# Order of the softmax work in a two-branch attention kernel: row maxima per bank, local exp split around the block exps, projection split around the first value group

## The reference

```python
q = rmsnorm(apply_partial_rope((h @ Wq_c @ Wq_up), cos, sin), q_norm_w)      # 16 heads
k_sw = rmsnorm(apply_partial_rope(h @ Wk, cos, sin), k_norm_w)               # one key head
v_sw = h @ Wv
ck = rmsnorm(h.reshape(b, nb, M * HID) @ W_comp, k_norm_w)                   # one key per 16 tokens
c_out = attend(q @ ck * scale, valid, sink, ck)                              # block branch
sw_scores = CAP * tanh((q @ k_sw * scale) / CAP)                             # CAP = 50
sw_out = attend(sw_scores, window of 64 tokens, sink, v_sw)                  # local branch
ao = c_out + sw_out
x = layernorm(h + (ao by groups @ Wg) @ Wo)
out = layernorm(x + x @ ternary(weight).T + bias)
```

## Time and profile before

| | us |
|---|---|
| median of 3 runs | 428.15 |
| the runs | 428.15, 428.4, 423.61 |
| the profiled execution, whole | 426.38 |
| its span, first to last instruction | 424.6 |
| busy: TensorE, VectorE, POOL, ScalarE | 367.8, 326.7, 302.3, 287.3 |
| mean granted TensorE clock, share of full speed | 0.965 |

### The profile page before, as it was taken

How to read it: one execution, slowest core, us unless ns; L and a number is a source line. 1 busy time by engine, 2 the same in 40 slices (tenths; PEclk the granted TensorE clock), 3 DMA queues, 4 the chain that set the end, 5 groups by cost and what they waited for, 6 DMA issues and landing times.

```text
span 424.6 us, 8753 instructions
## 1 busy us (share of the span) xinstructions
PE 367.8 (87%) x3109; PEld 297.5 (70%) x3111; DVE 326.7 (77%) x663; ACT 287.3 (68%) x818; POOL 302.3 (71%) x190
## 2 busy tenths in 40 slices
PE   5995798959979998999999999888889999989781
PEld 5993586656757767787878687767676877768660
DVE  2685789677888889897979787989886998963311
ACT  4557775767695969687777767686967695956200
POOL 1834361266796979798989777897979697986805
PEclk9998899978999999999999999999998999999995
DMA  7994004688756676767567676777676676584330
GB/s 248 316 247 112 1 0 67 233 247 124 124 91 123 100 138 95 130 101 121 106 112 103 107 110 108 114 110 139 97 127 100 115 100 125 87 137 76 47 66 25
DMA packets 150284, 50.20 MB, mean 118 GB/s; under 512 B 138593, under 2 KB 148833, under 8 KB 149985
## 3 DMA queue, kind: packets, MB, share of 16 engines
q1 hardware_dynamic: 149424, 49.32, 62.4%
q10 hardware_dynamic: 816, 0.33, 0.3%
HBM read 11.87 MB, written 4.19 MB: 38 GB/s over the span
## 4 chain that ended last, share of the span: by engine, by line
PE 33%; issue 17%; POOL 17%; DVE 11%; ACT 9%; DMA 7%; SPq 6%; POOLq 0%; ACTq 0%; DVEq 0%
PE PS L664 10%; POOL ao L1196 5%; PE PS L615 5%; POOL room_wg L1206 4%; SPq L373 4%; PE PS L641 3%; ACT room_h L822 3%; DMA aoT<-ao 3%; PE PS L471 3%; PE PS L633 3%; ACT ao L704 3%; PE PS L431 2%; PE PS L581 2%; DVE room_K L1112 2%; DMA room_h<-room_K 2%
## 5 line engine op out<-in xcount | busy, mean ns | idle before, releaser
L1196 POOL TENSOR_TENSOR ao<-room_wg,ao 128x1024 f16<-128x1024 f32 x32 | 68.2, 2132 | 28.0 <-ACT ao L704 27.9
L664 PE MATMUL PS<-V,room_wg 128*128 128x129 f32 x512 | 67.0, 285 | 13.7 <-POOL room_wg L1206 10.2
L664 PEld LDWEIGHTS PS<-V,room_wg 128*128 128x128 f32 x512 | 63.3, 197 | 18.8 <-POOL room_wg L1206 13.5
L1206 POOL TENSOR_TENSOR room_wg<-room_comp,keep 128x1024 f32<-128x1024 f32 x32 | 74.7, 2355 | 1.4 <-ACT room_comp L813 1.4
L822 ACT ACTIVATE room_h<-PS,room_K 128x8 f32<-128x8 f32 (+7 forms) x256 | 70.7, 364 | 1.9 <-DVE room_K L1047 1.7
L822 ACT ACTIVATION_READ_ACCUMULATOR room_h<-PS,room_K 128x1 f32 x256 | 62.4, 250 | 0.0
L633 PE MATMUL PS<-Weff,aoT 128*128 128x256 f16 x512 | 58.5, 273 | 3.8 <-DMA aoT<-ao 3.7
L1212 POOL TENSOR_TENSOR ny<-nx,nu 128x16 f32<-128x16 f32 x16 | 46.8, 2924 | 18.3 <-DVE nx L1023 18.3
L633 PEld LDWEIGHTS PS<-Weff,aoT 128*128 128x128 f16 x512 | 49.6, 98 | 10.8 <-issue 4.8
L1021 DVE TENSOR_REDUCE ssq<-room_wg 128x8 f32<-128x1024 f32 x30 | 36.5, 1220 | 21.9 <-ACT room_wg L773 21.5
L581 PE MATMUL PS<-room_h,kT 128*128 128x512 f16 x192 | 47.9, 391 | 4.2 <-ACT room_comp L809 2.4
(11 more groups left out here) (178 smaller groups left out, 734.5 us busy)
## 6 DMA issues: line engine op xcount, KB each, us to landing
H<-in_L_attn_h SPq DMA_DIRECT2D x4, 512.0 KB, 6.3
room_wg<-in_L_attn_Wg SPq DMA_DIRECT2D x1, 2048.0 KB, 14.7
cw_rows<-staged SPq DMA_DIRECT2D x1, 2048.0 KB, 6.4
CW<-cw_rows SPq DMA_DIRECT2D x1, 2048.0 KB, 7.9
aoT<-ao SPq DMA_TRANSPOSE x128, 2.7
out<-room_wo SPq DMA_DIRECT2D x16, 128.0 KB, 2.0
CW<-in_L_attn_Wq_up SPq DMA_DIRECT2D x2, 512.0 KB, 13.5
room_wo<-in_L_attn_Wo SPq DMA_DIRECT2D x1, 1024.0 KB, 15.2
```

The lines of the kernel that those rows point to most:

```text
L664: last = nc.tensor.matmul(pv, Pm[:, c, 2 * pr:2 * pr + 2, :], V[:, 2 * i + c, :], start=True, stop=True)
L1196: G.tensor_tensor(ao16[:, 1, c, :, :], ao[:, c, :, :], ao16[:, 0, c, :, :], ALU.subtract).then_inc(g_al, 1)
L1206: G.tensor_tensor(Pm[:, c, :, :], E[:, c, :, :], keep[:, :, :], ALU.mult).then_inc(g_mask, 1)
```

## The change

- Row maxima: the reduce is cut in two, `row_max(0)` for bank 4 and `row_max(1)` for bank 5. `row_max(0)` stands ahead of `rope_products(0)`, `row_max(1)` where the whole stood. `p_cs` and `d_cmax` count twice a step.
- ScalarE: the first local exp stays, then come the 16 block exps (the second eight wait for the second maxima), then the second local exp.
- x1's transposition goes from before the local scores to behind the second unit of them, where the step has attention; the narrowing of its tile from before the square to behind the first tanh.
- Projection: the blocks come first, then the high part of 16 - 2g heads, `values(0)`, the high part of the other 2g heads, the low part. In steps without attention all 16 heads come at once.

```diff
-                wait(sp, p_cs, t)
+                wait(sp, p_cs, 2 * t)
...
-                if ffn:
+
+                def norm_T():
                     pe.wait_ge(g_x1, i - 1)
...
                 if ffn and not mid:
+                    norm_T()
                     feed_forward()
...
                         last.then_inc(p_sw, 1)
+                        if ffn and u == 1:
+                            norm_T()
...
-                    last.then_inc(p_cs, 1)
+                        last.then_inc(p_cs, 1)
...
+                def project_blocks():
+
+                    pe.wait_ge(a_ct, t + 1)
+                    if t == 0:
+                        pe.wait_ge(s_cwr, 16)
+                    for g in range(groups(t)):
+                        rows = P - HEADS if g == groups(t) - 1 else P
+                        nc.tensor.matmul(o, PcT[0:rows, g, :], CW[0:rows, TPB * (t // TPB) + g, :],
+                                         start=g == 0, stop=False)
+
+                def project_high(heads):
+
+                    for hd in heads:
+                        if hd == 0:
+                            pe.wait_ge(s_ah, 64 * t + 64)
+                        for wp in range(2):
+                            nc.tensor.matmul(o, aoT[:, 0, hd % 2, hd // 2, :], Weff[:, wp, hd, :],
+                                             start=False, stop=False)
...
                 if proj:
 
                     t = i - 1
+                    ahead = HEADS - 2 * groups(t) if mid else HEADS
...
-                    if not mid:
-                        project_blocks(True, range(groups(t)))
-                    pe.wait_ge(s_ah, 64 * t + 64)
...
+                    project_blocks()
+                    project_high(range(ahead))
...
-                if proj and mid:
+                if proj:
+                    project_high(range(ahead, HEADS))
                     project_low()
-                    project_blocks(False, range(groups(t))).then_inc(p_o, 1)
                 if mid:
                     values(1)
...
                 if front and i < 1:
                     square(i + 1, 0)
-                if ffn:
-                    act.wait_ge(p_xt, i - 1)
-                    narrow(x1T[:, 0, :, :], x1_bank(mid).rearrange("p (k n) -> p k n", k=KC), a_xt)
                 if front:
                     square(i + 1, 1)
+                if ffn and not mid:
+                    feed_forward_high()
...
                                              ACT.Tanh, scale=1.0 / CAP).then_inc(a_tanh, 1)
-                    for c in range(2):
+                        if ffn and u == 0:
+                            feed_forward_high()
+
+                    def local_exp(c):
+
                         act.wait_ge(a_tanh, 4 * i + 2 * c + 2)
                         nc.scalar.activation(E[:, c, :, :], E[:, c, :, :], ACT.Exp, scale=CAP).then_inc(a_es, 1)
+
+                    local_exp(0)
...
-                    act.wait_ge(d_cmax, i + 1)
                     wait(act, p_ct, i)
                     n = SUB * groups(i)
                     for hd in range(HEADS):
+                        if hd % 8 == 0:
+                            act.wait_ge(d_cmax, 2 * i + hd // 8 + 1)
...
                             last.then_inc(a_ec, 1)
+                    local_exp(1)
...
+                def row_max(hf):
+
+                    dve.wait_ge(p_cs, 2 * i + hf + 1)
+                    wait(dve, a_ec, 2 * i)
+                    V_.tensor_reduce(mn[:, 8 * hf:8 * hf + 8], scores(i)[:, hf, :, :], AX.X, ALU.max,
+                                     negate=True).then_inc(d_cmax, 1)
+
+                if mid:
+                    row_max(0)
                 if front:
                     rope_products(0)
                 if first:
                     weights_rest(0)
                 if mid:
-
-                    dve.wait_ge(p_cs, i + 1)
-                    wait(dve, a_ec, 2 * i)
-                    V_.tensor_reduce(mn[:, :].rearrange("p (b a) -> p b a", b=2), scores(i), AX.X, ALU.max,
-                                     negate=True).then_inc(d_cmax, 1)
+                    row_max(1)
                 if front:
                     rope_products(1)
```

More of the change, by code:

```diff
@@ L604, in step @@
                 o = bank(7)[:, 0:HID]
[L606 to L624, removed]
-                    if not mid:
-                        project_blocks(True, range(groups(t)))
-                    pe.wait_ge(s_ah, 64 * t + 64)
-                def project_high():
-                    for hd in range(HEADS):
+                def project_blocks():
[10 more added lines that the diff above has]
+                            pe.wait_ge(s_ah, 64 * t + 64)
                         for wp in range(2):
-                            last = nc.tensor.matmul(o, aoT[:, 0, hd % 2, hd // 2, :], Weff[:, wp, hd, :],
-                                                    start=mid and hd == wp == 0, stop=False)
-                    return last
+                            nc.tensor.matmul(o, aoT[:, 0, hd % 2, hd // 2, :], Weff[:, wp, hd, :],
+                                             start=False, stop=False)
                 def project_low():
@@ L641, in project_low @@
                         last = nc.tensor.matmul(o, aoT[:, 1, hd % 2, hd // 2, :], Weff[:, 0, hd, :],
-                                                start=False, stop=not mid and hd == HEADS - 1)
-                    return last
-                if proj and mid:
[L646 to L649, removed]
+                                                start=False, stop=hd == HEADS - 1)
+                    last.then_inc(p_o, 1)
+                if proj:
+                    t = i - 1
+                    ahead = HEADS - 2 * groups(t) if mid else HEADS
+                    if i == 1:
+                        copied(pe, G_FT)
+                    wait(pe, d_y, t)
+                    project_blocks()
+                    project_high(range(ahead))
                 def values(c):
@@ L791, in step, with feed_forward_high @@
             def step(i, front, mid, proj, ffn):
+                def feed_forward_high():
+                    act.wait_ge(p_xt, i - 1)
+                    narrow(x1T[:, 0, :, :], x1_bank(mid).rearrange("p (k n) -> p k n", k=KC), a_xt)
                 if front and i < 1:
                     square(i + 1, 0)
-                if ffn:
-                    act.wait_ge(p_xt, i - 1)
-                    narrow(x1T[:, 0, :, :], x1_bank(mid).rearrange("p (k n) -> p k n", k=KC), a_xt)
                 if front:
                     square(i + 1, 1)
+                if ffn and not mid:
+                    feed_forward_high()
                 if i == -1:
```

## The result

| | before | after |
|---|---|---|
| median, us | 425.78 (22 runs) | 420.31 (22 runs) |
| lowest and highest, us | 421.28 to 432.4 | 417.04 to 427.62 |
| ratio | | 0.9897, 95% interval 0.9869 to 0.9926 |
| profiled execution, whole and span, us | 426.38 and 424.6 | 425.47 and 423.7 |

The account below looks back on a forecast made before the run. The loop was taken as bound by VectorE, then POOL, with TensorE tied in step 7. Terms -0.8 -0.5 -0.3 -0.5 +0.4 +0.6 = -1.1 us took 428.15 to 427.0 us, range 421.5 to 433.

Parts of the forecast that it names:

- one chain from a value group to the next: Step 3: VectorE, then POOL set the 19.1 us loop; no step of it waits for TensorE except the value group.
- Steps 1, 4 and 10, where a DMA came late too, are held by the mask.: Projection split: no gain counted in these steps, although the transposed ao came late there.
- Late ao: Projection split: blocks fill the wait for transposed ao, so value groups start earlier; -0.8 us in step 2, -0.5 in step 11.
- The stall: Value group's wait for block exps goes: -0.3 us in step 7, -0.5 in step 15, each less 0.2 for moved heads.
- Heads behind the group: Projection split: 0.025 us per group moves behind values(0), counting where y waits for the projection, four steps: +0.4 us.
- VectorE's hold: row_max(0) ahead of rope_products(0) holds VectorE for the first bank's scores: +0.6 us over six steps.
- The move of x1: x1's transposition behind the second score group: 0 taken, bounds 0 and -6.8 us.
- The late mask(1): POOL's mask(1) comes 0.4 to 1.3 us after mask(0) is done, waiting for the later exp; covered by other waits.
- TensorE is the bound: Rival: TensorE's waits for x1, exps and late ao all pay, 415.5 us; chance 0.10.
- The slow-clock rival: Late queries and half-clock scores, as in step 12, cost 2.4 us each; four such steps give 436.6 us; chance 0.08.

Follow-up runs that it names:

- the split alone: Kernel before with only the projection split (blocks first, some high heads and the low part behind the first value group): ratio 0.9962, 422.02 us against 424.93.
- The experiment on the low part alone: Kernel before with one swap: behind the first value group the blocks come before the low part; ratio 0.993.
- split and max+exp: Kernel before with the projection split, row maxima per bank and second local exp behind the block exps, without the move of x1: ratio 0.9878.
- both maxima behind: Changed kernel with both row maxima behind the first rope products, so that VectorE isn't held: ratio 0.9895, 420.19 us.
- the experiment on x1: Kernel before with only x1's transposition behind the second score unit and its narrowing behind the first tanh: ratio 1.0039.
- cover without balance: Like the projection split on the kernel before, but all 16 high heads stay ahead of the first value group: ratio 1.0041, 428.9 us.
- four pairs: All eight combinations of the three parts, four with the projection split against four without: mean 0.96% lower with it.
- max+exp: Kernel before with only the row maxima per bank and the second local exp behind the block exps: ratio 1.0034.
- the split with the exp alone: Kernel before with the projection split and second local exp behind the block exps, one reduce for all maxima: ratio 0.9984.

## Why the prediction was wrong

**One route where there are two.** The forecast followed one chain from a value group to the next: divide(0), query_rest, y, x1, POOL's work, mask(0). That is right for the steps from 3 to 4 and from 9 to 10, which stayed at 19.1 us with every part. There is a second from values(0): the low part, the blocks, values(1), the transposition of the block probabilities, its copy and a square on ScalarE, output_high(1), then POOL's output_low(1) and on. The first value group of step 4 starts at 165.70 us before. Behind it come the wait for the low part of ao, the second value group, y, and output_low(1):

```profile
168.08 1.92 PE L641 MATMUL PS<-Weff,aoT 128*128 128x256 f16 x16 [0.33 <-DMA aoT<-ao]
...
171.57 1.95 PE L664 MATMUL PS<-V,room_wg 128*128 128x129 f32 x16
171.89 0.47 DVE L1126 SCALAR_TENSOR_TENSOR room_wo<-PS,o_inv,H 128x256 f32<-128x256 f32 x1
...
177.07 2.13 POOL L1196 TENSOR_TENSOR ao<-room_wg,ao 128x1024 f16<-128x1024 f32 x1 [0.82 <-ACT ao L704]
```

The two value groups with the split alone:

```profile
164.40 2.05 PE L656 MATMUL PS<-V,room_wg 128*128 128x129 f32 x16 [0.76 <-POOL room_wg L1198]
169.79 1.95 PE L656 MATMUL PS<-V,room_wg 128*128 128x129 f32 x16
```

The first group waits 0.75 us for the mask in both, which is where I stopped: "Steps 1, 4 and 10, where a DMA came late too, are held by the mask." But the time between the two groups went from 5.87 to 5.39 us, and the step got 0.47 us shorter. The mask that holds step 5 comes by way of values(1) of step 4. The experiment on the low part alone shows that it is this route and not y's, for there the first value group starts within 0.04 us of the same time (165.66):

```profile
171.03 1.95 PE L664 MATMUL PS<-V,room_wg 128*128 128x129 f32 x16
171.85 0.47 DVE L1126 SCALAR_TENSOR_TENSOR room_wo<-PS,o_inv,H 128x256 f32<-128x256 f32 x1
...
176.53 2.13 POOL L1196 TENSOR_TENSOR ao<-room_wg,ao 128x1024 f16<-128x1024 f32 x1 [0.34 <-ACT ao L704]
```

y stands where it stood. values(1) is 0.54 us earlier, and so is output_low(1), before which POOL had been idle 0.82 us for ScalarE's ao and is now idle 0.34. A wait in the middle of a loop isn't proof that work behind it is free.

**Late ao, forecast -1.3, measured -2.9.** The mechanism and steps 2 and 11 were right: 1 to 2 gave 1.1 us for my 0.8, 10 to 11 gave 0.5 for 0.5. What I left out, with no term in the sum, is steps 4 and 12, 0.5 and (by estimate) 0.8. After, step 2 reads so:

```profile
125.84 1.03 PE L617 MATMUL PS<-CW,room_wo 128*128 128x256 f32 x4
...
127.36 2.79 PE L626 MATMUL PS<-Weff,aoT 128*128 128x256 f16 x24 [0.49 <-DMA aoT<-ao]
```

The blocks fill the wait (0.49 us left of the 1.72 in the earlier trace rows) and 24 matmuls are left for 32, in 2.79 us where I had worked out 2.8.

**The stall, forecast -0.8, measured -1.7.** Step 7 gave 0.54 for 0.3: the 0.55 that I had put there was right, and the 0.2 taken off it for the heads behind the group wasn't. Step 15 gave 1.17 for 0.5. The 0.7 that I had put there, less the same 0.2, stands in no row. The trace of before shows 0.93 us of idle time in the group, for the 0.29 of step 7, and the split alone still shows it:

```profile
389.97 0.71 PE L664 MATMUL PS<-V,room_wg 128*128 128x129 f32 x4 [0.93 <-ACT room_h L822]
...
385.49 0.71 PE L656 MATMUL PS<-V,room_wg 128*128 128x129 f32 x4 [0.96 <-ACT room_h L814]
```

**Heads behind the group, forecast +0.4 (and 0.2 twice in the stall's terms), measured 0.06 at most.** I divided 3.65 us by 32 matmuls and got 0.114. The last one's own 0.27 us doesn't count for spacing: (3.65 - 0.27) / 31 is 0.109, four of them 0.436, and a block group's two passes 0.433. The exchange is even. 8 to 9 is 20.75 before and 20.79 with the split.

**VectorE's hold, forecast +0.6, measured 0 to +0.3.** The hold is as large as worked out: 10.0 us over 17 waits, 0.6 each. Step 7 before, where two rows are missing in the earlier trace rows, and of the changed kernel (second profile):

```profile
226.37 1.61 PE L664 MATMUL PS<-V,room_wg 128*128 128x129 f32 x12 [0.38 <-POOL room_wg L1206]
...
233.59 1.95 PE L664 MATMUL PS<-V,room_wg 128*128 128x129 f32 x16
```

```profile
218.82 0.69 DVE L1052 TENSOR_REDUCE room_K<-PS 128x8 f32<-128x512 f32 x1 [0.62 <-PE PS L597]
...
224.17 2.05 PE L660 MATMUL PS<-V,room_wg 128*128 128x129 f32 x16 [0.56 <-POOL room_wg L1220]
...
225.49 2.35 POOL L1220 TENSOR_TENSOR room_wg<-room_comp,keep 128x1024 f32<-128x1024 f32 x1 [1.37 <-ACT room_comp L818]
...
226.85 0.22 DVE L1106 TENSOR_TENSOR dn<-PS,e 128x6 f32<-128x6 f32 x2
...
230.86 1.95 PE L660 MATMUL PS<-V,room_wg 128*128 128x129 f32 x16
231.06 0.48 DVE L1140 SCALAR_TENSOR_TENSOR room_wo<-PS,o_inv,H 128x256 f32<-128x256 f32 x1
```

From the value group divide(0) comes after 2.68 us, in the earlier trace rows after 2.65: VectorE gains nothing, as I had said. But values(1) comes after 6.69 us (it was 7.22: 233.59 less 226.37) and y after 6.89 (7.42 in the earlier trace rows). Both are TensorE's route, their 0.53 is the stall that is gone, and the step fell by 0.54. VectorE was full without being what the step waited for. In step 2 to 3 all three parts together cost 0.3 us, and the hold is its cause, for it went when both maxima stood behind the rope products. The 0.35 more in 14 to 15 (19.44 with split and max+exp, 19.45 in the first profile of the changed kernel, 19.42 with both maxima behind) isn't explained; the second profile doesn't have it.

**What held.** The move of x1: 0 forecast, and the wait for transposed queries took the place of the wait for x1, as the first of the two rows had hinted. The late mask(1): POOL stood 1.37 us before it and nothing came of that in the step. The rival "TensorE is the bound" (415.5) fell with the experiment on x1. The Trainium skill (Perfetto Trace Analysis, Identifying the Most-Contended Engine) says to go for the engine with the highest occupancy, and to judge TensorE not by its matmuls but by the busy share of its weight loads and its arithmetic. By the matmuls TensorE led by ten points; by the weight loads (70%) it stands behind VectorE's 77%. Taking 5.7 us of its waits away did nothing, while filling 3.3 us of other waits gave 3 by the steps. Which wait it is decides, and the share doesn't tell. The slow-clock rival didn't come: between step 1 and the last value group neither profile of the changed kernel has a half-clock stretch.

The sum as the steps show it, against a before of 308.2 us without its accident: -2.9 -1.7 + 0.3 (2 to 3) and -0.3 of small things, 303.6 us. That -4.6 lies within the interval of the ratio; with the first profile (305.2 us) it would be -3.0. A little of it may be the clock: the mean granted clock of the runs is 0.9672 before (89 runs) and 0.9692 after (34). A stretch like that of step 12, 14.7 us at half clock, takes 0.017 off the mean, so the 0.002 is one such stretch in nine runs, and at 1.3 us each some 0.15 us by this estimate.

## What to carry to other kernels

Where two routes lead from one event to the same event of the next round, price an edit on both. A wait shown at the end says which engine came last, and not that the route through the waiting engine is free. Put independent work in front of a late DMA, and move an equal amount behind, so that the engine reaches the shared point no later: cover without balance lost 1.7 us here, with balance it won 1.6 alone and 4 in the mean of four pairs. Whether savings ahead of a late transfer pay only once the transfer's wait is filled isn't shown: max+exp gained nothing alone by the whole times, but 0.7 us by the steps, and it and the move of x1 together gained 2 us without the split. When parts seem to need each other, look at the steps before the medians.

## What the runs showed of the hardware

With the same code most steps repeat their length within 0.1 us from kernel to kernel (in the two profiles of the changed kernel 13 of 16 do), while whole executions of one kernel spread over 10 us. The profiles show three sources of spread: the setup (the first value group began between 86.0 and 91.3 us), transposed queries that come later in one execution than in another (the three steps of the changed kernel where they did are 1.7 us longer), and stretches at half clock that come now and then: of 14 profiles one had such a stretch at the scores of step 12, and two, not of the changed kernel, at those of step 15. In one of these TensorE had been idle 1.99 us for x1 and 0.43 us for the transposed queries before it, and the twelve score matmuls took 4.45 us again:

```profile
375.92 0.44 PE L553 MATMUL PS<-ident,room_wo 128*128 128x128 f32 x2 [1.99 <-POOL room_wo L1228]
376.79 4.45 PE L581 MATMUL PS<-room_h,kT 128*128 128x512 f16 x12 [0.43 <-DMA room_h<-room_K]
```

That is the split with the exp alone; its step 14 to 15 took 21.96 us, where the profiles without such a stretch there have 18.8 to 19.9.
